# A feed-forward layer with ternary weights: the second token group moves from direct products to the seven-product scheme

## What is computed

```python
def _L0_ffn_ref(x, W_up, W_gate, W_down):
    wu, wg, wd = (ternary_quant(W) for W in (W_up, W_gate, W_down))   # clip(round(W / mean|W|), -1, 1) * mean|W|
    up = jnp.einsum('bsd,ed->bse', x, wu)          # 512 -> 2048
    gate = jnp.einsum('bsd,ed->bse', x, wg)        # 512 -> 2048
    hidden = jax.nn.silu(up) * gate
    return jnp.einsum('bse,de->bsd', hidden, wd)   # 2048 -> 512
...
x = x + 0.5 * _L0_ffn_ref(_layernorm(x, axis=-1), W_up, W_gate, W_down)
x = x + _L0_attn_ref(_layernorm(x, axis=-1), ...)
x = x + 0.5 * _L0_ffn_ref(_layernorm(x, axis=-1), W_up, W_gate, W_down)
```

## Time and profile before

| | us |
|---|---|
| median of 3 runs | 1810.19 |
| the profiled execution, its own time | 1809.33 |
| span of its trace | 1807.0 |
| TensorE busy | 1755.3 (97%) |
| VectorE busy | 1329.1 (74%) |
| ScalarE busy | 926.8 (51%) |
| GpSimd busy | 825.6 (46%) |

### The profile page before, as it was taken

The page is one execution under the profiler, slowest core; times in us unless marked ns, Lnnn a source line. Parts: engine busy times, 40 slices in busy tenths (PEclk is TensorE's granted clock), DMA queues, the critical chain, the costliest instruction groups (busy, mean ns, idle before and its releaser), DMA issues. The chain is left out here.

```text
span 1807.0 us, 35150 instructions
## 1 busy us (share of the span) xinstructions
PE 1755.3 (97%) x13070; PEld 1266.9 (70%) x13070; DVE 1329.1 (74%) x2294; ACT 926.8 (51%) x1391; POOL 825.6 (46%) x553
## 2 busy tenths in 40 slices
PE   6999999999999999999999999999999999999998
PEld 3465888888888844444444444555888888888887
DVE  6838887778875857786786786657787778877655
ACT  7614457465473545445445445435447465474553
POOL 0496444363353515555455455536244362452533
PEclk9999999999999999999999999999999999999999
DMA  7032121311114030212212211111121311112100
GB/s 325 1 94 42 47 42 47 87 41 47 47 41 140 0 102 26 63 36 61 61 35 61 61 35 44 54 64 42 47 42 47 87 39 48 41 47 64 41 24 23
DMA packets 132968, 103.82 MB, mean 57 GB/s; under 512 B 100880, under 2 KB 100880, under 8 KB 131088
## 3 DMA queue, kind: packets, MB, share of 16 engines
q1 hardware_dynamic: 132880, 102.81, 18.9%
HBM read 49.59 MB, written 25.17 MB: 41 GB/s over the span
## 5 line engine op out<-in xcount | busy, mean ns | idle before, releaser
L493 POOL TENSOR_TENSOR f_hlo<-f_h,f_hhi 128x768 f16<-128x768 f32 x135 | 201.9, 1496 | 616.5 <-ACT f_hhi L663 588.3
L1146 PE MATMUL f_down_ps<-wd,f_hhi 128*128 128x256 fp8e4 x1440 | 318.5, 273 | 3.1 <-DVE xa L872 3.1
L1146 PE MATMUL f_down_ps<-wd,f_hlo 128*128 128x256 fp8e4 x1440 | 318.5, 273 | 0.0
L1219 PE MATMUL f_gate_ps<-spare 128*128 128x256 f16 x2496 | 306.2, 272 | 0.2 <-issue 0.2
L1219 PEld LDWEIGHTS f_gate_ps<-spare 128*128 128x128 fp8e4 x2496 | 236.2, 97 | 41.5 <-issue 0.4
L1219 PE MATMUL f_up_ps<-spare,wu 128*128 128x256 f16 x1664 | 213.5, 273 | 0.1
L872 DVE SCALAR_TENSOR_TENSOR xa<-f_down_ps,out_scale,xa 128x512 f32<-128x512 f32 x195 | 136.3, 743 | 60.3 <-PE f_down_ps L1146 60.0
L1219 PEld LDWEIGHTS f_up_ps<-spare,wu 128*128 128x128 fp8e4 x1664 | 160.2, 98 | 21.6 <-issue 0.3
L1146 PEld LDWEIGHTS f_down_ps<-wd,f_hhi 128*128 128x128 f16 x1440 | 140.6, 98 | 21.9 <-issue 5.1
L1591 POOL TENSOR_TENSOR s_am<-s_tri,s_al 128x512 f16<-128x512 f16 x128 | 153.1, 1225 | 6.1 <-DVE s_al L1851 6.1
L1146 PEld LDWEIGHTS f_down_ps<-wd,f_hlo 128*128 128x128 f16 x1440 | 140.7, 98 | 16.2
(11 more groups left out here) (241 smaller groups left out, 3302.6 us busy)
## 6 DMA issues: line engine op xcount, KB each, us to landing
res<-xa SPq DMA_DIRECT2D x16, 1024.0 KB, 4.3
xa<-res SPq DMA_DIRECT2D x16, 1024.0 KB, 5.4
xa<-in_u SPq DMA_DIRECT2D x8, 1024.0 KB, 5.6
xa<-res SPq DMA_DIRECT2D x32, 256.0 KB, 2.6
res<-xa SPq DMA_DIRECT2D x32, 256.0 KB, 2.0
spare<-in_w_up SPq DMA_DIRECT2D x4, 1024.0 KB, 10.6
late<-in_w_gate SPq DMA_DIRECT2D x4, 1024.0 KB, 17.9
late<-in_w_in SPq DMA_DIRECT2D x1, 2320.0 KB, 8.7
```

What stands on the lines that cost most here:

```text
L493: last = nc.gpsimd.tensor_tensor(hlo[:, p, a:b, :], src, hhi[:, p, a:b, :], ALU.subtract)
L1146: last = nc.tensor.matmul(at, part[:, p, kind, m * P:(m + 1) * P], wd[:, weight, p, :], start=(p == 0 and part is hhi and (m == 0 or name ...
L1219: last = nc.tensor.matmul(acc[:, j * HT:(j + 1) * HT], w[:, k, e * P:(e + 1) * P], xop[part][:, o, k, :, :], start=(fresh and (j, k, part) ...
```

## The change

- `NC` is 1 in both passes. Group 1 of the first pass runs in `seven`; `turn`, `normalize_rows`, `low_rows`, `high_rows` and their semaphores are gone.
- The row sums of group 1 are made from step 14 of group 0 on; those of group 2 follow, between the additions of group 0's down tiles. VectorE's list after step 15 is: `rows_low(1,0)`, `rows_start(1,1)`, `rows_sums(1,1)`, four statistics of group 2, `rows_low(1,1)`, variance of group 2, add tile 0, add tile 1, `rows_start` and `rows_sums(2,0)`, add tile 2, `rows_low(2,0)`, `rows_start`, `rows_sums` and `rows_low(2,1)`, add tile 3. ScalarE makes `rows_high` of (1,0) ahead of silu 15, and (1,1), (2,0), (2,1) ahead of `seven(1)`.
- GpSimd: weight sums 0 and 1 after low part 3 of group 0, 2 after 4, 3 after 5; then, after low part 7, sums 4 to 6, inverse deviation of group 2, sum 7, the four down-weight sums, sums 8 to 11; sums 12, 13 and 14, 15 after `p` 0 and 1 of `seven(1)`.
- Down weight in group 0: the absolute sum of quarter 1 moves to VectorE (whole, after step 4), those of quarters 0, 2, 3 stay on ScalarE after steps 1, 5 and 7; the scale is made at step 9 instead of 8; two of four own masks become signs on ScalarE; pieces are spread anew.
- In group 0's down product the last two `p` (before: the last one) come after both first tiles' other `p`. Some buffers move (`b12`, `own_masks`).

```diff
-                NC = 2 if first else 1
+                NC = 1
...
-                N_TERN, T_EARLY, T_AFTER = len(TERNARY), 9, (1, 1, 1, 1, 1, 2, 1, 2, 1, 2, 1, 2, 1, 1, 1, 0)
+                N_TERN, T_EARLY, T_AFTER = len(TERNARY), 9, (1, 1, 1, 1, 1, 2, 1, 2, 1, 2, 2, 2, 1, 1, 0, 0)
-                OWN = [n for n, (w, q, e0, e1) in enumerate(TERNARY) if n < 5 or (w == 2 and e0)]
+                OWN = [n for n, (w, q, e0, e1) in enumerate(TERNARY) if n < 5 or (w == 2 and e0 and q % 2 == 0)]
...
+                    if first and (g, p) == (1, 0):
+                        eng.wait_ge(t_done, 2)
...
-                        S_EARLY = 10
+                        S_EARLY = 12
                         def direct_group():
                             for p in range(HK):
                                 if p == 5:
+                                    inv_std(1)
                                     pool.wait_ge(tern_done, 2 + AT_DOWN[0])
-                                if p == 6:
-                                    inv_std(1)
...
+                                if p == 3:
+                                    pool.wait_ge(tern_done, AT_DOWN[0])
+                                for i in {3: (0, 1), 4: (2,), 5: (3,)}.get(p, ()):
+                                    s_sum(i)
+                            for i in range(4, 8):
+                                if i == 7:
+                                    inv_std(2)
+                                s_sum(i)
                             t_sums()
-                            for i in range(S_EARLY):
+                            for i in range(8, S_EARLY):
                                 s_sum(i)
...
+                            seven(1, 3, {0: (12, 13), 1: (14, 15)})
...
                             for i in range(KE):
+                                if i == KE - 1:
+                                    rows_high(1, 0)
                                 if i > 3:
                                     silu(0, i)
+                                if i and i % 2 == 0:
+                                    hid_high_direct(i // 2 - 1)
                                 for n in pieces_after(i):
                                     if n not in OWN:
                                         sign(n)
-                                if 1 <= i <= 4:
-                                    abs_sum(2, i - 1)
-                                if i and i % 2 == 0:
-                                    hid_high_direct(i // 2 - 1)
+                                if i in (1, 5, 7):
+                                    abs_sum(2, {1: 0, 5: 2, 7: 3}[i])
                             hid_high_direct(HK - 1)
-                            high_rows(1, 0, CH)
+                            rows_high(1, 1)
+                            for c in range(2):
+                                rows_high(2, c)
...
+                                if i == 4:
+                                    abs_whole(2, 1)
...
+                                if i == KE - 2:
+                                    rows_start(1, 0)
+                                    rows_sums(1, 0)
+                            rows_low(1, 0)
+                            rows_start(1, 1)
+                            rows_sums(1, 1)
+                            for c in range(CH):
+                                stats(2, c)
+                            rows_low(1, 1)
+                            dve.wait_ge(stat_done, after(3 * CH))
+                            variance(2)
+                            add_tile(0)
+                            add_tile(1)
+                            rows_start(2, 0)
+                            rows_sums(2, 0)
+                            add_tile(2)
+                            rows_low(2, 0)
+                            rows_start(2, 1)
+                            rows_sums(2, 1)
+                            rows_low(2, 1)
+                            add_tile(3)
...
                             for t in range(2):
-                                down_tile_of(t, 0, HK - 1)
+                                down_tile_of(t, 0, HK - 2)
                             for t in range(2):
-                                down_tile_of(t, HK - 1, HK)
+                                down_tile_of(t, HK - 2, HK)
...
-                                if i == 8:
-                                    pe.wait_ge(tern_done, 1 + pieces_after(7)[-1])
+                                if i == 9:
+                                    pe.wait_ge(tern_done, pieces_after(8)[-1])
                                     weight_sum(2)
```

More of the change, by code:

```diff
@@ L195, in ffn_part @@
                     masks = [flat_hi[:, 49 * HT:49 * HT + 1024], flat_lo[:, 51 * HT:51 * HT + 1024]]
-                    b12 = late[:, 4736:4736 + HK * HE // 4].bitcast(F8).rearrange("p (k d) -> p k d", k=HK)
+                    b12 = behind[:, 0:HK * HE // 4].bitcast(F8).rearrange("p (k d) -> p k d", k=HK)
                     raw_g = late[:, :]
-                    own_masks = [spare[:, 512 * i:512 * (i + 1)].bitcast(F16) for i in range(2)]
+                    own_masks = [spare[:, 4096 + 512 * i:4096 + 512 * (i + 1)].bitcast(F16) for i in range(2)]
                     wsum = sb(ctx, "wsum", [P, 3, 6])
@@ L405, in _ @@
                     def _(sp):
[L406 to L416, removed]
                         def turn_sums(g):
@@ L445, in _ @@
                             load(1, u_v, 1)
-                            turn(1)
                             sp.wait_ge(tern_done, N_TERN)
@@ L542, in group, with seven @@
                                     inv_std(g + 2)
-                                if first and p in (0, 1, HK - 1):
-                                    s_sum(S_EARLY + p % 5)
-                            if first:
-                                for i in range(S_EARLY + 3, 16):
-                                    s_sum(i)
-                        def seven(g, ln):
+                        def seven(g, ln, between={}):
                             for p in range(HK):
@@ L554, in seven @@
                                     inv_std(ln)
+                                for i in between.get(p, ()):
+                                    s_sum(i)
                         if first:
@@ L558, in _ @@
                             direct_group()
-                        group(NC - 1)
-                        with pool.Fori(NC, NG - 2) as g:
+                            seven(1, 3, {0: (12, 13), 1: (14, 15)})
+                        else:
+                            group(0)
+                        with pool.Fori(NC + first, NG - 2) as g:
                             seven(g, g + 2)
@@ L601, in copy_transposed @@
                             nc.scalar.activation(xnt[:, k, :], tr_ps[k % 2][:, :], ACT.Copy).then_inc(xlo_done[k % 2], 1)
-                        def high_rows(g, c0, c1):
-                            for c in range(c0, c1):
-                                if c == 0:
-                                    act.wait_ge(turned, after(32 * g))
-                                    act.wait_ge(tern_done, 1 + AT_DOWN[3])
-                                act.wait_ge(norm_done, after(CH * g + c + 1))
-                                nc.scalar.activation(xnh[:, c, :], tr_ps[c % 2][:, :], ACT.Copy, scale=XS).then_inc(xnh_done, 1)
                         def rows_high(g, c):
@@ L788, in normal, with normalize @@
                                                            rstd[:, c:c + 1], ALU.subtract, ALU.mult)
[L790 removed]
+                        def normalize(g, dst):
                             dve.wait_ge(rstd_done, after(g + 1))
[L792 to L812 removed]
+                            for c in range(CH):
+                                last = normal(g, c, dst[:, c, :])
+                            last.then_inc(xn_done, 1)
                         def rows_start(g, c):
```

85 lines of the change are left out of this document (29 added, 56 removed).

## The result

The changed kernel takes 1822.8 us (median of 4 runs, 1821.5 to 1824.8) against 1810.2: a ratio of 1.007, 95% interval 1.0057 to 1.0082, so slower by 12.6 us; forecast were 1822.4. Its profiled execution took 1824.84 us with a span of 1823.1, 16.1 more than before; it is the slowest of the four.

What follows compares the result with a forecast made beforehand. TensorE was taken as the bound, with VectorE and ScalarE pacing group 0's steps. −11.7 + 4.3 + 3.6 + 8.4 + 8.5 = +13.1 on 1809.33 gave 1822.4 us; own range 1814 to 1829, widened to 1802 to 1829.

Steps and rivals of the forecast that it cites:

- Part 1: Group 1 in seven products instead of direct: 85.4 us becomes 73.7, −11.7, of which 6.9 is fewer columns.
- Part 2: Steps of group 0: VectorE's longer list and locked waits delay steps 12 and 14; +4.3 us, ends +1.5 and +5.
- Part 3: Down product of group 0: tile 2 waits some 6 us for add tile 0 behind VectorE's row sums; +3.6, ends −0.9 and +4.
- E: The time at which the steps of group 0 end, forecast at 86.5 us.
- Part 4: Start of group 1: TensorE waits for group 2's rows, held up beside GpSimd's down-weight sums; +8.4, ends 7.0 and 9.7.
- V: The time at which the variance of group 2 is done on VectorE, forecast at E + 19.1 us.
- Part 5: Weight sums 12 to 15 inside `seven(1)` hold up the pair sums: 4.7 and 3.8 us, +8.5; ends 2.9 and 9.
- the locked waits are absent: Rival: VectorE's waits for GpSimd's current instruction are mostly hidden or absent; sum −8.2, 1801.1 us; chance 0.17.
- they cost only at the down-weight sums: Rival: VectorE's waits for GpSimd cost only beside the down-weight sums; sum −1.2, 1808 us, no change; chance 0.13.
- The clock: Rival: TensorE's clock falls in two new waits of about 6 us, some 2 us each; 1826 us; chance 0.08.

Runs made afterwards that it cites:

- e6: Changed kernel with every down-weight sum on GpSimd cut into four instructions and every weight sum into two, same work and order; 1818.2 us.
- e5: Changed kernel with GpSimd's weight sums 0 and 1 moved behind low part 6 of group 0, and 2 and 3 behind low part 7; 1824.0 us.
- e1: Changed kernel with the four down-weight sums cut to 16 of 256 columns, the rest cleared to zero by GpSimd at the start; 1819.5 us.
- e10: The order of e9 with whole sums, one instruction each, instead of cut ones; 1814.9 us.
- e3: Changed kernel with 70 unused filler matmuls on TensorE ahead of the first product of group 1; 1821.1 us.
- e2: Changed kernel with weight sums 12 to 15 made ahead of group 1's low parts instead of after `p` 0 and 1; 1816.7 us.
- e4: Changed kernel with 32 unused filler matmuls on TensorE ahead of down tile 2 of group 0; 1823.6 us.
- e8: e7 with add tile 0 ahead of `rows_low(1,1)` and weight sums 0 to 5 later in group 0's steps; 1817.0 us.
- e7: e6 and e2 together on the changed kernel: cut sums, and weight sums 12 to 15 ahead of group 1's low parts; 1815.9 us.
- e11: e9 with add tile 0 moved ahead of `rows_low(1,1)`, as in e8; 1808.7 us.
- e9: e7 with three weight sums moved into GpSimd's gaps in group 0's steps and the first down-weight sum ahead of the inverse deviation; 1811.4 us.

## Why the prediction came out right

The median is met within 0.4 us, and the mechanism on which it rests, VectorE held up beside GpSimd, is shown. The parts are less exact than that: in the trace they add up to 15.2 us instead of 13.1, and the median rose by 12.6 only because the profiled execution of after lies 2.0 over its median and that of before 0.9 under it. Of the five terms one is right throughout; the other four are near in size, but in each of them something that was left out took the place of something too large.

**Part 1, −11.7.** Right: 93.1 us less the two waits (13.9) are 79.2, and of these 5.1 are slow clock (2.3 behind P5 and 2.8 behind the pair sums), which leaves 74.1 for the 73.7 forecast.

**Part 2, +4.3, measured +3.6.** The steps ended at 85.8, 86.5 forecast. Step 12 came at 69.24 after one wait of 3.94, earlier than 70.3 to 71, and step 14 did not wait at all: the walk put too much into VectorE's list. At full clock the steps would have ended at 83.0, 3.4 before the forecast. In place of these 3.4 the clock stood at 0.50 for at least 4.8 us, which costs half of that and a little more behind it, some 2.7. In e6 the same wait of 3.95 us brought no slow clock:

```profile
69.30:74.00 4.70, 4.65 (x22) 2.05 (x23) 4.67 (x10) 2.11 (x3) 2.29 (x3) 1.00 0.00 0
```

and its tile 2 started 2.3 us earlier (101.30 against 103.59), though its shorter sums have a share in that. The step that failed is the length of VectorE's list at steps 12 and 14; that a small `tensor_tensor` is held is shown (1.68 us for one number, 0.16 in e5). The evidence on group 0's pace was read too broadly as well: of the five waits in the earlier trace rows only two, of 2.4 us, lie in group 0, the other three in group 1.

**Part 3, +3.6, measured +3.9.** The variance was done at E + 17.1 instead of + 19.1 (the steps as listed add up to 20.0), so tile 2 waited 3.7 us, not 6. Most of the 3 us of waiting at `rows_start` and `rows_sums(1,1)` did not come: weight sum 4 began only at 95.47, when the last of them, L805 at 94.86, had begun, and that one took 0.93. Then tiles 2 and 3 took 16.6 us instead of 14.05, at a clock of 0.50 at first. Again the sum holds by two errors of opposite sign. The transposes were no bound, as said.

**Part 4, +8.4.** The wait was 9.35, inside the 7 to 9.7, but it is another one. The prediction let TensorE wait for ScalarE's copy behind P1 and then for VectorE's first sum. It overlooked that P5 of `p` 0, which comes before the copy is needed, waits until the low parts of four row chunks, the two of group 1 and the two of group 2, are made (`rl_done`, L817). ScalarE's copy was done at 127.71, VectorE's last low part at 131.20. The size came out because the second of the two forecast waits stood at the end of the same VectorE list: add tile 3 at V + 26.5 to 29.4, measured V + 29.0. The forecast left out the clock behind this wait, 2.3. e1 (−6.7 us of this wait with short sums), e6 (−6.0 with short holds) and e10 (−2.0 with whole sums in an earlier place) show that the holds of the down-weight sums make it; e3 shows that a busy TensorE does not shorten it.

**Part 5, +8.5, measured 7.4** (a wait of 4.6 and 2.8 of slow clock)**.** The first wait is right instruction by instruction: 2.18, 2.22 and 1.85 for three pair sums and 4.59 for TensorE, 4.7 forecast. The second, 3.8 at `p` 2, did not come: TensorE's half clock behind the first had made it late by 2.8 us, and sums 14 and 15 were over by then; in e1 and e6, where that slow stretch cost 1.3 and 1.5, it came, with 2.3 and 2.6 us. e2 gives the sum of both, 6.1 in the median and 8.3 in the trace.

**The rivals.** That the locked waits are absent is refuted by e1, e2 and e6, that they cost only at the down-weight sums by e2. The clock, held at 0.08: it fell in four waits, of 3.7 to 9.4 us, 10.3 us in all (2.7, 2.5, 2.3, 2.8), of which e4 shows the 2.5 of tiles 2 and 3 to lie off the path. The argument against it, that no stage of the earlier trace rows shows a low clock, was empty: no stage there had such a wait. Its price, 2 us for each wait, came near the 2.3 to 2.8 measured by luck: the granted clock of before in 20.3 to 26.0 us, where its row of 5.84 us stands, is 1.00. The Trainium skill, page TensorE: Matmul & The Clock Gate, section HAM oscillation, says that waits of this order throttle the engine again and again, and on this the trace of after agrees; that of e8, below, does not. Waits were forecast too long at three places (3.4 at steps 12 and 14, 2.3 at tile 2, 3.8 at `p` 2), 9.5 together, and the slow clock that was left out comes to 10.3 at its four places, 7.8 without the one that e4 takes off the path: that the sum fits is luck in part. The forecast's own range does not follow from its terms: the ends named for its parts give 1812.6 to 1824.9, not 1814 to 1829 (and part 5's low end is two times 1.6, that is 3.2 instead of 2.9). The model also had no term for the length of GpSimd's list, and forecast e7 at 1808 to 1811 where it took 1815.9.

What stays open: why e11 starts group 2 4.4 us before e9 but lies only 2.7 under it in the median, and why the clock fell behind the wait of step 12 in after and in the ten other traces and not in e6 and e7.

## What to carry to other kernels

Before work is moved beside a busy GpSimd, mark VectorE's instructions with two inputs in SBUF, and its `tensor_scalar` from SBUF to SBUF, and count one GpSimd instruction of waiting for each; cutting the GpSimd sums of 4 us in four took 6.0 us from the wait at P5 here (e6), nearly as much as leaving most of their work out (6.7, e1). Then add up the lists themselves between two hand-overs: once the holds were short, GpSimd's 37 us of sums were the bound, and only filling its gaps helped. And where a forecast has TensorE wait a few us, look for the clock behind the wait, since a trace without waits says nothing on it.

## What the runs showed of the hardware

A GpSimd instruction that only writes held VectorE as well: the clear of 6.9 us in e1 made four normalises of 1.92 us last 8.48. The Trainium skill, page SBUF — State Buffer, section Who interferes with whom, names `tensor_scalar` among the instructions that can contend with GpSimd for the shared port pair, and the row agrees. Size did not save a `tensor_tensor`: one of 128x1 took 1.68 us in after (0.16 alone). But three `tensor_scalar` of 128x1 just ahead of it (L1009 twice, L1014) took 0.15, 0.14 and 0.15 beside the same weight sums, and were not held. Nor were four `bn_stats` with one input in SBUF: 2.46 us beside weight sums, 2.47 at the start of before, where GpSimd is idle.

```profile
61.89 0.15 DVE L1014 TENSOR_SCALAR scale<-total 128x1 f32<-128x1 f32 x1
62.08 1.68 DVE L1039 TENSOR_TENSOR prod<-scale 128x1 f32<-128x1 f32 x1
```

A `tensor_tensor` with one input in PSUM was not held. In e10, where a down-weight sum of 4 us began at 107.81:

```profile
105.12 3.02 DVE L774 TENSOR_SCALAR spare<-xa,f_mv,f_rstd 128x512 f32<-128x512 f32 x1
108.17 0.43 DVE L803 TENSOR_TENSOR f_tr_ps<-spare,f_tr_ps 128x256 f32<-128x256 f32 x1
108.51 3.60 DVE L804 TENSOR_TENSOR f_tr_ps<-spare 128x256 f32<-128x256 f32 x1
```

The middle one reads one operand from PSUM and runs inside that sum at 0.43; of the other two, one goes from SBUF to SBUF and one has both inputs in SBUF, and both are held to the end of a sum.

The clock after a wait did not follow from its length. After 3.9 us it was 0.50 in after and 1.00 in e6, at the same matmul of step 12. At P5 of `p` 0 it fell to 0.75 on average behind 2.64 us in e3, and stayed at 1.00 behind 3.91 us in e8:

```profile
118.06 1.03 PE L1223 MATMUL f_tr_ps<-spare 128*128 128x256 f16 x8 [3.91 <-DVE late L825]
118.94 1.04 PE L1223 MATMUL f_gate_ps<-spare 128*128 128x256 f16 x8
```

It did not always fall at once either. In e1, behind 2.69 us, eight matmuls ran at full speed (1.03 us), and only the next ones slowly:

```profile
129.91 1.77 PE L1216 MATMUL f_gate_ps<-spare 128*128 128x256 f16 x8
```
